# Gating the mixing layer's rows on VectorE, and the first experts written out on TensorE

## The reference, cut to what matters

```python
# layer 0, experts: each expert e works on the rows that chose it
hmid = einsum('ech,ehi->eci', dispatch, wi); hmid = gelu(hmid)      # 256 -> 1024
eout = einsum('eci,eih->ech', hmid, wo)                             # 1024 -> 256
x = x + gb * einsum('tec,ech->th', combine_weights, eout)

# layer 1, mixing layer on h = modulated layernorm of x
Xn = layernorm(h) * gamma + beta
Q, K, V = split(Xn @ W_in + b_in)
K, V = rotary(K), rotary(V)
A = 0.5 * sum_over_rows(cos_sim(K) * cos_sim(V)) + 0.5              # one row of 256 numbers
x = x + ga * ((A * Q) @ W_out + b_out + h)
```

## Time and profile before

| | |
|---|---|
| median of 3 executions | 1107.87 us (1106.48 to 1108.92) |
| the profiled execution | 1109.56 us |
| its span, first to last instruction | 1107.8 us |
| TensorE busy | 974.3 us, 88% of the span |
| VectorE busy | 636.7 us, 57% |
| ScalarE busy | 521.1 us, 47% |
| GpSimd busy | 305.0 us, 28% |
| mean granted TensorE clock | 0.943 |

### The profile page before, as it was taken

One profiled execution on the slowest core, in us unless ns is written; L12 is line 12 of the kernel. 1 busy time (PEld: TensorE's weight loads), 2 busy tenths in 40 slices (PEclk: granted clock), 3 DMA queues, 4 the chain that ended last, 5 costly groups with the idle time before them and its releaser, 6 DMA issues. The chain is left out here.

```text
span 1107.8 us, 24791 instructions
## 1 busy us (share of the span) xinstructions
PE 974.3 (88%) x9939; PEld 634.4 (57%) x9943; DVE 636.7 (57%) x1642; ACT 521.1 (47%) x813; POOL 305.0 (28%) x348
## 2 busy tenths in 40 slices
PE   7789899999999999886499999858867699999993
PEld 4333334444444444443277777646554699999993
DVE  5568999999799888655600000277475633333331
ACT  4433567777865876755122121276335233333330
POOL 2100510011011111230142432237540245554541
PEclk9988999999999999998699999979888799999997
DMA  5880000000000000006834686121323023222324
GB/s 186 181 169 4 3 2 2 3 3 2 2 3 2 3 2 3 3 2 227 278 94 125 183 252 183 20 76 49 123 78 132 24 46 50 47 47 48 47 43 95
DMA packets 63276, 78.81 MB, mean 71 GB/s; under 512 B 12097, under 2 KB 54977, under 8 KB 62737
## 3 DMA queue, kind: packets, MB, share of 16 engines
q1 hardware_dynamic: 50688, 61.54, 18.5%
q0 software_dynamic: 11968, 15.47, 8.6%
q10 hardware_dynamic: 528, 0.52, 0.1%
HBM read 58.12 MB, written 21.36 MB: 72 GB/s over the span
## 5 line engine op out<-in xcount | busy, mean ns | idle before, releaser
L594 ACT ACTIVATE k_prob<-f_s 128x1024 f32<-128x1024 f32 (+3 forms) x320 | 270.1, 896 | 121.6 <-PE f_s L432 120.9
L654 DVE TENSOR_REDUCE k_mpart<-f_r 128x1 f32<-128x512 f32 x384 | 250.5, 685 | 34.6 <-PE f_r L375 32.3
L375 PE MATMUL f_r<-k_ks,k_qs 112*32 112x512 bf16 (+3 forms) x2560 | 210.8, 357 | 20.8 <-DMA k_qs<-q_dram 8.2
L432 PE MATMUL f_s<-k_qs,k_ks 114*32 114x512 bf16 (+3 forms) x2560 | 174.1, 350 | 1.9 <-ACT k_prob L594 1.3
L850 POOL TENSOR_SCALAR_AFFINE_SELECT k_prob<-k_prob 128x256 f32<-128x256 f32 x128 | 51.5, 408 | 383.6 <-ACT k_prob L594 382.4
L375 PEld LDWEIGHTS f_r<-k_ks,k_qs 112*32 112x32 bf16 x2560 | 68.6, 95 | 138.6 <-DVE k_mpart L654 56.0
L448 PE MATMUL f_o<-k_prob,k_vaug 128*32 128x512 f32 (+3 forms) x1280 | 145.9, 530 | 1.5 <-POOL k_prob L850 1.4
L651 DVE CUSTOM_DVE_ANT_0 k_unread<-f_r,k_causal 128x128 bf16<-128x128 f32 (+3 forms) x256 | 121.1, 484 | 18.3 <-PE f_r L375 17.2
L432 PEld LDWEIGHTS f_s<-k_qs,k_ks 114*32 114x32 bf16 x2560 | 63.9, 97 | 79.8 <-issue 28.5
L2210 DVE TENSOR_TENSOR mid<-silu_g,e_u 128x512 f32<-128x512 f32 x39 | 26.8, 687 | 111.6 <-PE e_u L2112 110.7
L1348 DVE SCALAR_TENSOR_TENSOR outr<-p_o,k_w,k_mod 128x256 f32<-128x256 f32 x16 | 7.7, 484 | 134.5 <-PE p_o L1283 134.5
(11 more groups left out here) (391 smaller groups left out, 1287.5 us busy)
## 6 DMA issues: line engine op xcount, KB each, us to landing
k_w1T<-in_L_ffn_w_dram SPq DMA_DIRECT2D x18, 512.0 KB, 10.6
k_w1T<-in_L_ffn_wi_dram SPq DMA_DIRECT2D x8, 1024.0 KB
k_w1T<-in_L_ffn_wo_dram SPq DMA_DIRECT2D x8, 1024.0 KB
k_qs<-q_dram SPq DMA_DIRECT2D x6, 768.0 KB, 10.1
h_rows<-k_h SPq DMA_DIRECT2D x8, 512.0 KB, 4.6
sum<-k_x SPq DMA_DIRECT2D x8, 512.0 KB, 6.3
q_dram<-k_room SPq DMA_DIRECT2D x12, 256.0 KB, 9.3
k_rot_t<-in_L_ffn_w_dram SPq DMA_DIRECT2D x6, 512.0 KB, 5.0
```

The lines of the kernel that those rows point to most:

```text
L375: last = nc.tensor.matmul(dst[32 * j:32 * (j + 1), :], qs[0:KROWS, c, GH * g + hs, q0:q0 + 32], ks[0:KROWS, QC * ck:QC * ck + w], start=Tr ...
L432: last = nc.tensor.matmul(sc[h % 2][32 * j:32 * (j + 1), i, off:QC], ks[0:KALL, k0:k0 + 32], qs[0:KALL, c, GH * g + 2 * pair + i, off:QC], ...
L594: nc.scalar.activation(prob[:, u % 2, 2 * pair:2 * pair + 2, off:QC], sc[h % 2][:, :, off:QC], ACT.Exp, scale=HD ** -0.5).then_inc(e_done, 1)
L654: nc.vector.reduce_max(mpart[:, s % 2, hs, t, ck:ck + 1], bank(r)[:, 0:w], AX.X).then_inc(ring_used[r % RING], 1)
```

## The change

In **layer 0's experts** the drain after each expert goes, and with it `slot_free`; SyncE waits on `o_done` instead, which the expert's last matmul counts up. The loop of TensorE goes: all eight experts are written out. The offsets of two go too, and with them ScalarE's and VectorE's counting up at the start. ScalarE keeps its loop.

In the **mixing layer** GpSimd's three `add_gated` go to VectorE: the gating of quarters 0, 1, 2 stands behind tiles 5, 8, 11 (`gate_rows`), and the addition behind tiles 6, 9, 12 (`add_rows`). The last quarter's pair moves from before the sum to behind `w_sc`. The three operations on `w_out`, `bq` and `b_out` move from behind tile 7 to behind `A_rows` (the first two) and behind `w_sc` (`b_out`). GpSimd waits once for all four additions before it adds the bias.

```diff
@@ phase_experts0
             for e in range(2, E):
-                sp.wait_ge(slot_free, e - 1)
+                sp.wait_ge(o_done, NST * (e - 1))
                 load_weights0(sp, k, a, e, e % 2)
...
                 for n in range(NI):
-                    pe.wait_ge(gelu_done, e * NI + n + 1)
+                    if e * NI + n >= 2:
+                        pe.wait_ge(gelu_done, e * NI + n - 1)
...
                     last.then_inc(o_done, 1)
-                pe.drain().then_inc(slot_free, 1)
 
             transposes(0, 0)
-            with pe.Fori(0, E // 2 - 1) as i:
-                expert(i, 0, True)
-                expert(i, 1, True)
-            expert(E // 2 - 1, 0, True)
-            expert(E // 2 - 1, 1, False)
+            for e in range(E):
+                expert(e // 2, e % 2, e + 1 < E)
@@ phase_mix, GpSimd
-                if i in (3, 6, 9):
-                    add_gated(i // 3 - 1)
...
+            pool.wait_ge(gated, NC)
             pool.wait_ge(wc_ready, 2)
@@ phase_mix, VectorE
             for i in range(TQ, NT):
                 products(i)
-                if i == 2 * TQ - 1:
-                    tt(w_out[:, :, :], w_out[:, :, :], bcast(gate, KH), ALU.mult).then_inc(wout_ready, 1)
-                    tt(b_out[:, :], b_out[:, :], gate, ALU.mult).then_inc(wout_ready, 1)
-                    nc.vector.tensor_copy(bq_rep[:, :, :], last_bcast(bq[:, :], P)).then_inc(wout_ready, 1)
-
-            last = NC - 1
-            dve.wait_ge(normal_h, NC)
-            step(tt(quarter(k.h, last), quarter(k.h, last), bcast(gate, TQ), ALU.mult))
-            tt(quarter(k.x, last), quarter(k.x, last), quarter(k.h, last), ALU.add).then_inc(last_gated, 1)
+                if i in (5, 8, 11):
+                    gate_rows(i // 3 - 1)
+                if i in (6, 9, 12):
+                    add_rows(i // 3 - 2)
+
             dve.wait_ge(A_done, 1)
...
             tt(out[:, :, 1], A_sum[:, :], A_dif[:, :], ALU.subtract).then_inc(Arow_ready, 1)
+            tt(w_out[:, :, :], w_out[:, :, :], bcast(gate, KH), ALU.mult).then_inc(wout_ready, 1)
+            nc.vector.tensor_copy(bq_rep[:, :, :], last_bcast(bq[:, :], P)).then_inc(wout_ready, 1)
             dve.wait_ge(A_done, 2)
             nc.vector.tensor_scalar(A[:, :], pAt[:, :], 0.25, 0.5, ALU.mult, ALU.add).then_inc(A_ready, 1)
             dve.wait_ge(A_ready, 1)
+            dve.wait_ge(wout_ready, 1)
+            nc.vector.tensor_scalar(w_sc[:, 0, :], w_out[:, 0, :], A[:, 0:1], None, ALU.mult).then_inc(wsc_ready, 1)
+            tt(b_out[:, :], b_out[:, :], gate, ALU.mult).then_inc(wout_ready, 1)
+            gate_rows(NC - 1)
+            add_rows(NC - 1)
             dve.wait_ge(wout_ready, 3)
-            nc.vector.tensor_scalar(w_sc[:, 0, :], w_out[:, 0, :], A[:, 0:1], None, ALU.mult).then_inc(wsc_ready, 1)
             dve.wait_ge(wc_done, 1)
```

More of the change, by code:

```diff
@@ L1276, in expert @@
                     transposes(i + s, 1 - s)
-                pe.wait_ge(gelu_done, e * NI + NI + 2)
+                pe.wait_ge(gelu_done, (e + 1) * NI)
                 for r, (r0, rn) in enumerate(RT):
                     b = (3 * s + r) % 2
-                    pe.wait_ge(o_copied, e * 3 + r + 1)
+                    if e * 3 + r >= 2:
+                        pe.wait_ge(o_copied, e * 3 + r - 1)
                     for n in range(NI):
@@ L1308, in _ @@
         def _(act):
[L1309 to L1310 removed]
+            nc.scalar.activation(unread[:, :], k.rstd[:, 0:1], ACT.Gelu)
             with act.Fori(0, E // 2) as i:
@@ L1363, in _ @@
                     b = NST * e + r
-                    pool.wait_ge(o_copied, b + 1 + 2)
+                    pool.wait_ge(o_copied, b + 1)
                     dst, width = (k.sum0, D) if rn == P else (halves, P)
@@ L2029, in _ @@
             last.then_inc(wc_done, 1)
+            pe.wait_ge(wout_ready, 2)
             for m in range(KH):
```

24 lines of the change are left out of this document (9 added, 15 removed).

## The result

| | before | changed |
|---|---|---|
| median of 6 executions each, same chip | 1107.66 us (1106.48 to 1109.66) | **1093.92 us** (1091.58 to 1096.53) |
| ratio of the two | | 0.987, 95% interval 0.9852 to 0.9889 |
| the profiled execution | 1109.56 us | 1093.71 us |
| its span | 1107.8 us | 1092.0 us |
| mean granted TensorE clock | 0.943 | 0.945 |

The changed kernel is 13.7 us faster (12.3 to 16.4 by the interval). The forecast was 9.2 us. The two profiled executions differ by more than the medians, 15.8 us, since the one of before was 1.9 us above its median.

A forecast was written before the change was run, and what follows sets the result against it. TensorE, busy 88% of the span, was taken as the bound, with gains only from its pauses. Experts -5.0 and mixing layer -4.2 gave -9.2 us: 1107.87 - 9.2 = 1098.7 us, range 1095.2 to 1102.2.

The forecast's parts named there:

- 0.05 us left per passage: Experts: idle time TensorE was assumed to keep at each of seven passages, turning 5.4 us of pauses into 5.0 gained.
- The passages between experts: Layer 0's experts: removing drains, looping and register arithmetic ends TensorE's seven pauses ahead of `p_h`, -5.0 us.
- The passage itself holds: Rival, experts: narrow matmuls and head waits keep the pauses; 1.5 us gained in place of 5.0, 1102.2 us; chance 0.12.
- The drain of the eighth expert saves nothing: End of the experts: no gain from the last drain, since GpSimd's own drain of 3.72 us sets the barrier.
- GpSimd relieved: Mixing layer: without its six gating operations, GpSimd lets the last sum start 3.95 us behind the last keys, not 6.37; -2.4 us.
- The pause of 1.92 us: Mixing layer: TensorE's stop, laid to three VectorE operations behind tile 7, goes when they leave the tiles; -1.9 us.
- Gating on VectorE, 0.1 us: Mixing layer: six operations inserted among VectorE's tiles fit in its idle time, at a cost of 0.1 us.
- nothing late behind the sum: Mixing layer, after the last sum: operations moved there are covered by VectorE's waits; cost zero, without cover up to 0.5 us.
- rival: The clock stays up through the shorter pause before the last sum: 2.1 us more gained, 1096.6 us; chance 0.28.
- The mixing gain is eaten: Rival, mixing layer: insertions stop TensorE by 0.5 us each at five places, making keys late; 1101.2 us; chance 0.10.
- VectorE becomes the bound: Rival, mixing tiles: six uncovered insertions of 2.9 us each add 17.3 us on TensorE, giving 1116.0 us; chance 0.03.
- The clock: Pause before the last sum: the granted clock falls again and costs the same as before, 0 us.

The follow-up runs named there:

- before_as_control: The kernel before, unchanged, compared with itself: 1105.40 us, ratio 1.0 (0.9983 to 1.0016).
- drain_only: The kernel before without the experts' drain and its semaphore, loop and arithmetic kept: 1098.91 us, ratio 0.9949.
- block_moved_gating_stays: The kernel before with only the operations on `w_out`, `bq` and `b_out` moved behind `A_rows`, gating left on GpSimd: 1106.32 us, ratio 0.9998.
- gating_moved_block_stays: The kernel before with only the gating moved to VectorE; the operations on `w_out`, `b_out` and `bq` stay behind tile 7: 1102.64 us, ratio 0.9963.
- no_gating: The changed kernel with the four gating operations and four additions left out, so it computes less: 1095.53 us, ratio 0.9904 to the kernel before.
- whole_again: The changed kernel, unchanged, compared a second time with the kernel before: 1094.98 against 1106.16 us, ratio 0.9901.
- whole_third_time: The changed kernel, unchanged, compared a third time with the kernel before: 1095.31 against 1105.28 us, ratio 0.9906.

## Why the prediction was right and wrong

**Where the sum failed.** The step that failed stands in its last line: 9.2 us of terms for the change were set against one median, and the code that the change leaves alone stood in the sum, and in the range, with nothing. In the two profiles 2.9 us of the difference stand ahead of the experts and 0.8 behind the output matmuls' start, where no code changed. The same two kernels, compared again, differ by 11.0 and 10.4 us, not 13.7. A second step, smaller, is the 0.05 us left per passage. Which stretches were fast in the executions that made up the first medians is not known, since only one of each was profiled.

**The passages between experts: mechanism right, size taken from an unusual profile.** Forecast -5.0, of 5.4 us of pauses. In the two profiles the starts of `p_h` moved by 5.1 us over six passages; with the first, taken at the 0.76 us of its like, that is 5.8. The 0.05 us left per passage are wrong: nothing is left. But the 5.4 us came with drains of 1516 ns. With the 1298 ns of the later profiles the starts move by 3.8 us over six passages (116.66 in `before_as_control`, 112.84 in the changed kernel), with the first 4.3, so there the forecast was 0.7 too high. That 5.0 lies between the two is luck. The rule of the Trainium skill (TensorE: Matmul & The Clock Gate, Part 3) on row groups, by which the gain would have been 3.1 us, is not borne out by these traces. The prediction quoted one half of that section; by the other half, a load into the background weight buffer goes ahead too. The 18.81 us of every passage agree with that half. And a pause in the timeline is a little less than what the expert loses to it (1.08 us against 19.95 - 18.81 = 1.14). "The passage itself holds" falls with `drain_only`.

**Drain, arithmetic, branch.** The prediction shared each pause out among the three, and each share was there: 0.40 us for the branch, by the pauses of 0.86 and 0.46. But the shares do not go one by one: without the drain the other two vanish with the loop in place. Writing the loop out was worth 2 us beside a drain and 0.2 us without. The sum was not hurt, since all went together.

**The drain of the eighth expert saves nothing: right.** The last scatter stands 19.4 us behind the last `p_h` in both profiles. The 0.9 us at the barrier come from its landing, 5.1 us before GpSimd's drain in one and 4.25 in the other. Over all profiles the stretch from the first of the twelve turned halves to the mixing layer is 9.2 to 9.7 us with drains and 8.4 to 9.5 without, so most of this may be variation.

**GpSimd relieved: right.** Forecast 3.95 us from the last keys to the last sum, -2.4; measured 4.01, -2.4.

**The pause of 1.92 us: size right, its place in the sum wrong.** It went, as forecast, and the block's leaving would have been enough for that. But the prediction gave the block a term of its own, 1.9 us beside GpSimd's 2.4. `block_moved_gating_stays` shows that the move of the block was worth nothing by itself, and `gating_moved_block_stays` that the move of the gating was worth the whole 4.1 us, since GpSimd's gating had stretched the block. The row for it was already among mine, the copy's 2.44 us. I used it to price the insertions, and did not ask what the block would take without the gating beside it. The Trainium skill (SBUF — State Buffer, section SBUF: two separate sides, on the shared port pair) says that the loser waits for a whole instruction. The copy agrees, since it ends 0.16 us behind the gating, though with its one input it is not the case that the prediction quoted. The first two insertions and GpSimd's turns beside them agree as well (1.70 in place of 1.21, 1.64 in place of 0.72). The power does not. By the rule an insertion that meets it was to take 2.9 us (estimate of the prediction); the one at 758.18 started inside the power of 757.85 and took 1.21, and the one at 768.13, inside the power of 767.76, took 1.21 too. There the measurement decides.

**Gating on VectorE, 0.1 us, and nothing late behind the sum: right.** `no_gating` puts the first at zero. The wait ahead of the first addition is 0.56 us before and after. "The mixing gain is eaten" and "VectorE becomes the bound" are false: no pause on `m_vals` follows an insertion.

**The clock: forecast and rival each had some of it.** I had it fall again and cost the same. (The pause was forecast at 3.05 us; the prediction's own terms give 3.95 less the 1.00 us of the sum before it, 2.95. It is 3.02.) In the changed kernel it fell within the sum, and 1.49 us in place of 1.94 for the sum itself makes up the 0.4 us that the stretch behind it gained. Windows of its profile:

```profile
777.00:778.00 1.00, 0.23 (x4) 0.19 (x8) 0.00 (x0) 0.00 (x0) 0.59 (x2) 1.00 0.23 76
778.00:779.00 1.00, 1.00 (x8) 0.00 (x0) 0.00 (x0) 0.00 (x0) 0.00 (x0) 0.64 1.08 383
779.00:780.00 1.00, 1.00 (x8) 0.82 (x5) 0.67 (x4) 0.00 (x0) 0.00 (x0) 0.50 1.09 379
```

In `whole_again` it fell right behind the sum, for some 3.4 us of work (before, 4.3). In `whole_third_time` it did not fall, and TensorE's timeline shows what came in its place:

```profile
781.57 1.06 PE L1982 MATMUL m_pA<-k_w1T,m_w_tok 128*32 128x512 f32 x8 [3.02 <-issue]
...
786.53 0.66 PE L902 MATMUL m_pw<-k_ident,k_rot_t 128*128 128x128 f32 x4 [0.66 <-DMA k_rot_t<-in_L_ffn_w_dram]
```

From the sum to the output matmuls it took 10.23 us, against 11.35: so the rival is worth 1.1 us and not 2.1, in part since a faster TensorE meets the transfer of the weights (0.66 us). The pause is 3.02 us in all three profiles of the changed kernel, so its length alone does not say whether the clock falls.

**The range.** It took in the unknown costs of the change, but not that two executions of unchanged code differ: 7 us ahead of the experts, 1.5 us in the drains, 1 us at the barrier. Of the 6.6 us by which the two profiles differ more than forecast, 2.9 stand ahead of the experts, 1.0 in the first expert beside its passage, 0.9 at the barrier, 0.8 in the passages, 0.2 in the mixing layer up to the output (4.4 against 4.2), and 0.8 behind it. The later comparisons, at 10 to 11 us, would have stood inside the range: 1107.87 - 11.0 = 1096.9. What remains open is why the clock in the attention comes back at different times, and whether the longer drain belongs to a chip or to an execution: one of the six profiles with these drains shows it.

## What to carry to other kernels

A drain costs more than its own tail: it also lays bare the loop's branch and arithmetic, which cost nothing without it, so look for a semaphore on the last instruction before writing out a loop. When an operation is moved off GpSimd, take again the price of everything that VectorE ran beside it, and ask of each pause whether it alone holds the end of the stretch. Before a change's own bounds, put into the range what identical code differs by from one execution to the next, read from a second profile of the same kernel.

## What the hardware showed that I had not expected

- A branch and the register arithmetic of a loop on TensorE cost nothing between matmuls without a drain (18.81 us per expert, looped or written out; ahead of the loop 0.2 us); with one they cost about 0.2 us for the arithmetic and 0.4 us more where the loop goes round, on top of 0.31 us for the drain.
- The passage from 64-column matmuls to full-width ones costs nothing, although the opposite one idles the weight loads for 0.33 us.
- A VectorE copy of 256 numbers per row took 2.44 us beside GpSimd's operation on 1024 numbers, and 0.28 beside its power.
- A VectorE operation on two inputs of 1024 numbers took 1.70 us when it started behind a GpSimd turn, and 1.21 when it started ahead of one or inside a power.
- TensorE's drain took 1516 ns in one profile and 1298 in the five others that have it.
- In unchanged code the mean granted clock of one stretch of 50 us was between 0.69 and 0.83, and what follows started up to 7.1 us apart.
